# A two-layer transformer block on one core: the order of the jobs at the front of layer 0 and in the last expert run of layer 1

## The reference

```
h = layernorm(x) * (1 + ca) + sa
x = x + ga * attention(h)
h = layernorm(x) * (1 + cb) + sb
x = x + gb * experts(h)
```

```
for e in range(16):
    h = silu(xf @ W1[e] + b1[e]) * (xf @ W11[e] + b11[e])
    y = y + (h @ W2[e] + b2[e]) * gates[:, e, None]
z = silu(xf @ Ws1 + bs1) * (xf @ Ws11 + bs11) @ Ws2 + bs2
return y + z
```

## Time and profile before

| what | us |
|---|---|
| median of 3 executions | 1346.05 |
| lowest and highest of the 3 | 1339.43 and 1347.36 |
| the profiled execution, its own time | 1335.45 |
| its span, first to last instruction | 1333.7 |
| busy: PE, PEld | 973.1, 578.1 |
| busy: DVE, ACT, POOL | 844.6, 583.3, 437.7 |
| mean granted TensorE clock | 0.857 |

### The profile page before, as it was taken

One profiled execution on the slowest core, in us unless ns is written; L12 is line 12 of the kernel. 1 busy time (PEld: TensorE's weight loads), 2 busy tenths in 40 slices (PEclk: granted clock), 3 DMA queues, 4 the chain that ended last, 5 costly groups with the idle time before them and its releaser, 6 DMA issues.

```text
span 1333.7 us, 17366 instructions
## 1 busy us (share of the span) xinstructions
PE 973.1 (73%) x5741; PEld 578.1 (43%) x5741; DVE 844.6 (63%) x1977; ACT 583.3 (44%) x1409; POOL 437.7 (33%) x624
## 2 busy tenths in 40 slices
PE   5561374994985996887787888887877786877683
PEld 3231132452453564343334543444555553545573
DVE  1388888769989432566677656665655676635654
ACT  3334252453443243255454534434555553565253
POOL 0201342634635123022443232416312248423412
PEclk9775595996988998698799978768999997999787
DMA  7300000001000000000000000003144304242354
GB/s 229 102 0 0 1 0 1 1 0 36 1 1 1 0 1 25 23 1 0 1 1 1 1 0 1 1 0 129 55 116 125 87 25 148 77 123 66 129 179 119
DMA packets 54313, 60.40 MB, mean 45 GB/s; under 512 B 6208, under 2 KB 40656, under 8 KB 54224
## 3 DMA queue, kind: packets, MB, share of 16 engines
q1 hardware_dynamic: 52176, 55.10, 13.9%
q0 software_dynamic: 2048, 4.20, 1.1%
HBM read 46.05 MB, written 13.24 MB: 44 GB/s over the span
## 4 chain that ended last, share of the span: by engine, by line
PE 49%; DVE 21%; ACT 12%; issue 10%; POOL 6%; DMA 1%; SPq 0%; DVEq 0%; another core or an unknown queue 0%; POOLq 0%; ACTq 0%
PE banks L779 8%; PE banks L836 4%; PE banks L922 4%; PE banks L826 4%; DVE MX L1431 3%; PE banks L614 3%; PE banks L789 3%; POOL oms L1930 3%; PE banks L666 2%; PE banks L854 2%; PE banks L792 2%; PE banks L896 2%; ACT PT L1747 2%; ACT yh L1682 2%; PE banks L861 1%
## 5 line engine op out<-in xcount | busy, mean ns | idle before, releaser
L1431 DVE TENSOR_REDUCE MX<-banks 128x4 f32<-128x512 f32 (+2 forms) x192 | 199.2, 1043 | 89.6 <-PE banks L896 84.2
L1907 POOL TENSOR_SCALAR_AFFINE_SELECT PT<-PT 128x256 f32<-128x256 f32 x256 | 106.6, 430 | 405.5 <-ACT PT L1747 405.4
L1747 ACT ACTIVATE PT<-banks 128x768 f32<-128x768 f32 (+1 forms) x192 | 168.0, 878 | 108.1 <-PE banks L854 106.0
L779 PE MATMUL banks<-xgT,wg 128*128 128x128 f32 x616 | 87.8, 289 | 39.2 <-ACT ysb L1708 36.5
L861 PE MATMUL banks<-KS,QS 32*128 32x512 f32 (+3 forms) x512 | 98.0, 427 | 20.0 <-DVE MX L1431 15.7
L826 PE MATMUL banks<-w,hid 128*128 128x128 f32 x512 | 77.5, 299 | 45.2 <-DVE hid L1376 42.9
L922 PE MATMUL banks<-PT,VA 128*17 128x512 f32 (+3 forms) x1024 | 98.2, 483 | 16.2 <-DVE on L1454 10.8
L854 PE MATMUL banks<-QS,KS 32*128 32x128 f32 (+3 forms) x512 | 94.0, 412 | 14.1 <-ACT PT L1747 8.4
L826 PEld LDWEIGHTS banks<-w,hid 128*128 128x128 f32 x512 | 70.0, 207 | 78.8 <-DVE hid L1376 60.4
L779 PEld LDWEIGHTS banks<-xgT,wg 128*128 128x128 f32 x616 | 76.9, 197 | 51.9 <-issue 49.9
L1380 DVE SCALAR_TENSOR_TENSOR sil<-sil,yh 128x256 f32<-128x256 f32 x109 | 47.7, 438 | 62.5 <-ACT sil L1688 54.7
(11 more groups left out here) (273 smaller groups left out, 2100.2 us busy)
## 6 DMA issues: line engine op xcount, KB each, us to landing
wg<-in_ffn_dram SPq DMA_DIRECT2D x77, 386.0 KB
yb<-ysb SPq DMA_DIRECT2D x17, 256.0 KB, 3.9
xg<-xs SPq DMA_DIRECT2D x16, 256.0 KB
w<-in_ffn_w_dram SPq DMA_DIRECT2D x12, 256.0 KB
xs<-zt SPq DMA_DIRECT2D x2, 1472.0 KB, 14.2
xs<-zt SPq DMA_DIRECT2D x1, 1984.0 KB, 12.8
x<-in_L_attn_x_dram SPq DMA_DIRECT2D x4, 256.0 KB, 5.9
out_dram<-x SPq DMA_DIRECT2D x16, 64.0 KB
```

Of the source, the lines that this page charges most:

```text
L779: mm = e.matmul(ps[:, at:at + cols], w, h, start=True, stop=True)
L1431: v_mx.at(e.tensor_reduce(MX[n % 2][:, u:u + nm, qb % 2, 2 * pair:2 * pair + 2, 24].rearrange("p s i -> p i s"), p4, AX.X, ALU.max, negate ...
L1747: a_p.at(e.activation(PT[q % 3][:, 2 * pair:2 * pair + 2, :], where["score", q, pair][:, :, 0:n], ACT.Exp, scale=ISQ8))
L1907: ins = e.affine_select(out=pt, in_=pt, compare_op=ALU.is_ge, fill=0.0, base=0, pattern=[[0, 2], [1, 128]], channel_multiplier=-1)
```

## The change

At the front, `mod(1)` and the second group's jobs get other times, and `diag` is cut in three, each with its own signal: `diag(w)` writes four matrices, and `conv(g, w)` waits for w + 1 of them instead of for all. In the tail, the shared units 4 to 7 of the last batch move behind the first four tiles of the run, and the unit numbers and the banks follow. The gap in the table between chunk 0 and the other chunks grows from 6 to 10, and `turn(2, 0)` moves ahead on the scale.

```diff
@@ moe1_table
     for j in range(SHARED):
-        table += [(e + first + every * j, ("up", 1, n, j)), (e + first + 6.5 + every * j, ("down", 1, n, j))]
+        t = e + first + every * j if n < 3 or j < 4 else e + 70 + 2.1 * j
+        table += [(t, ("up", 1, n, j)), (t + 6.5, ("down", 1, n, j))]
...
-        gap = 6.0 if picked and c else 0.0
-        table.append((a - (2 if c != picked or not picked else 1.5) + step * tiles[0] + gap if c >= picked else e + 57,
+        gap = 10.0 if picked and c else 0.0
+        table.append((a - (2 if c != picked or not picked else 1.5) + step * tiles[0] + gap if c >= picked else e + 54.6,
@@ table_layer0
-    table = [(0.0, ("mod", 0)), (5.0, ("mod", 1))] + input_table(0, 1.0) + input_table(1, 6.0) + [(19.0, ("diag",))]
+    table = [(0.0, ("mod", 0)), (SCAN[0] + 1, ("mod", 1))]
+    table += [(1.0, ("stat", 0, 0, (0, 0))), (4.0, ("norm", 0, 0, (0, 0))), (5.0, ("stat", 0, 1, (0, 1))),
+              (7.2, ("norm", 0, 1, (0, 1)))]
+    table += [(8.0 + 4 * g + w, ("qkv", g, w)) for g in range(2) for w in range(3)]
+    table += [(12.5 + w, ("diag", w)) for w in range(3)] + [(24.0, ("ab", 0)), (28.0, ("ab", 1))]
@@ numbers of the units
-            return 16 * n + j if l == 0 else SHARED0[n] + j if j < SHARED else RUN0[n] + j - SHARED
+            if l == 0:
+                return 16 * n + j
+            if j >= SHARED:
+                return run_unit(n, j - SHARED)
+            return SHARED0[n] + j + (4 if n == 3 and j >= 4 else 0)
+
+        def run_unit(g, j):
+
+            return RUN0[g] + j - (4 if g == 2 and j < 4 else 0)
@@ conv on TensorE
-                pe.wait_ge(a_dg, 1)
+                pe.wait_ge(a_dg, w + 1)
@@ up on TensorE
-                    if j >= SHARED:
+                    if j >= SHARED and n < 2:
                         pool += (5,)
-                    i = pool[j % len(pool)]
+                    i = pool[(u if len(pool) == 5 else j) % len(pool)]
@@ diag on ScalarE
-            def diag():
+            def diag(w):
...
-                for j in range(12):
+                for j in range(4 * w, 4 * w + 4):
```

More of the change, by code:

```diff
@@ L498, in unit @@
         def unit(l, n, j):
-            return 16 * n + j if l == 0 else SHARED0[n] + j if j < SHARED else RUN0[n] + j - SHARED
+            if l == 0:
[5 more added lines that the diff above has]
+            return RUN0[g] + j - (4 if g == 2 and j < 4 else 0)
         def tile_unit(t):
             g = max(g for g in range(3) if TILE0[g] <= t)
-            return RUN0[g] + t - TILE0[g]
+            return run_unit(g, t - TILE0[g])
         def top_index(quarter, qb, u, pair):
@@ L1699, in turn @@
                     before, c0 = (g, c - 2) if c > 1 else (g - 1, len(CHUNKS[g - 1]) + c - 2)
-                    a.wait_ge(p_p3, RUN0[before] + CHUNKS[before][c0][-1] + 1)
+                    a.wait_ge(p_p3, run_unit(before, CHUNKS[before][c0][-1]) + 1)
                 a_xg.at(e.activation(xgT[cc % 2][:, 0:128 * m], where["turn", g, c][:, 0:128 * m], ACT.Copy))
@@ L1704, in keep @@
                 cc = CHUNK0[g] + j // 4
-                u = RUN0[g] + j
+                u = run_unit(g, j)
                 a.wait_ge(p_y, u + 1)
```

## The result

The changed kernel takes 1324.86 us in the median of 20 runs (1315.1 to 1332.53); the kernel before, measured with it, 1341.46 us in 20 runs (1329.09 to 1348.8). The ratio is 0.9888 with a 95% interval of 0.9865 to 0.9912, so 15.0 us less (11.8 to 18.1); the two medians are 16.6 us apart, the two means 15.0. Forecast were 18.1 us less and 1328 us. The profiled execution of the changed kernel has a span of 1322.9 us.

What follows compares the result with a forecast made beforehand. No engine is full; TensorE's serial jobs bound the front, idle time and low clock the tail. Front -7.6 and tail -10.5 sum to -18.1 us: 1328 from the 1346.05 median (profiled 1317.4), range 1317 to 1341.

Steps and rivals of the forecast that it cites:

- The front: Start of the kernel to the scan: convolutions' last transposes 10.6 us sooner, 3.0 given back, net 7.6 us less.
- the whole give-back: Behind the first scan step: VectorE waits for mod(1)'s products, delaying group 2's statistics and later scan steps; costs 3.0 us.
- B: Front: TensorE's clock stays low through all three convs, 5.9 us less gain, 1334 us in total; chance 0.12.
- D: Front: late x of group 1 or weights cw hold the chain, scan still pays 3.0; 1338.5 us; chance 0.09.
- The turn: Tail: turn(2, 0) goes with the parts of PT and ends at 1258.3 instead of 1263.87, 5.5 us sooner.
- The second half of the tail: From the turn's end to tile 8's `up`: 5 of the tail's 10.5 us, from filled idle time and faster clock.
- the other 5: Tail behind the turn: 3.12 us of idle time filled with work, and 1.9 us of clock on tiles 0 to 3.
- the 2.44 us: Tail: unexplained VectorE wait ahead of hid at 1268.65, taken to go with the second idle time.
- rival C: Tail: VectorE's wait returns, tiles 0 to 3 stay slow, a weight is late; 5.3 us less gain, 1333; chance 0.15.
- Rival E: Last run: with five banks, each tile's `up` waits for ScalarE's ysb; slower, up to 1353 us; chance 0.06.
- what would show it right: Front and tail marks: conv(0, 0) near 23, no 3 us idle, clock 1.00 behind the turn, tile 8's `up` 10.5 sooner.
- signs of being wrong: Front, scan and tail: convs of 5.4 us, `up` released by ysb, tiles waiting for weights, scan over 3.5 us longer.

Runs made afterwards that it cites:

- the turn alone: Changed kernel's front plus only the sooner turn(2, 0), all eight shared units ahead of tile 0 as before; mean 1324.1 us against 1341.3 for the kernel before.
- chips X and Z: Two follow-up groups, front or tail variants and unedited repeats, all profiles with stops; the changed kernel took 1340.3 and 1341.5 us, the kernel before 1346.9 and 1349.2.
- front alone: Only the front edits, with the tail of the kernel before: 1340.0 us against 1346.9 in one group, 1345.6 against 1349.2 in another.
- chip Y: Follow-up group of four kernels with the new front and sooner turn, no stops in their profiles: 1322.1 to 1325.7 us against 1341.3 for the kernel before.

## Why the prediction was right, and where it was not

**The front: right, term by term.** conv(0, 0) at 22.90 for a forecast of 22.85; its time 3.68 for 3.46; the last transposes at 37.75 for 37.7; VectorE's idle time 2.34, and the whole give-back 10.56 - 7.65 = 2.9 for 3.0. (The parts written down for the 3.0, products of 1.4 to 2.7 us and 0.55 us on VectorE from 73.94 on, give 1.5 to 2.8; that it met 2.9 is in part luck.) Over all profiles, step 45 is at 181.8 in the mean of nine with the new front and mod(1) as changed, and at 189.4 in three with the old: 7.6 us, the number forecast. Rivals B and D are out, by the convs of 3.7 and 3.5 us and by the start. Not tried was each of the three edits of the front by itself.

**The turn: right.** From the first operation on PT to xgT it is 6.83 us instead of 12.95, so 6.1 us for a forecast of 5.5, and at the low clock as expected; 0.5 us more were to be had with the clock.

**The second half of the tail: right in size, by luck, and wrong in its reason.** The forecast took 10.5 us to tile 8's `up`, and the first two profiles show 11.2 (11.57 less the 0.33 by which VectorE's first operation on PT came sooner); 10.5 are left at the last ysb, most of the difference being the wait for weights ahead of tile 13. The forecast had taken everything from tile 8 on as shifted; these 0.7 us are the exception. But the step that read "the other 5 are the second idle time of 3.12 that has work in it now, and 5.68 - 3.81 = 1.9 of clock" was not what happened. With the turn alone, in the old order of units, both are gone as well on a chip without stops, and 10.4 of the 11.3 us at the fifth ysb are there: 6.1 of the turn, 2.4 of a stop that did not come, 1.9 of clock. The step that failed is the sentence on the 2.44 us: "I can't explain; I let it go with the idle time". It was the trace of a stop: VectorE's hid waits there for TensorE's count p_y, which rises at 1268.53, where the records end the three `down` at 1266.07. And it does not go with the idle time: on chips X and Z the new order meets it with more behind it, and takes 38.2 us to the fifth ysb where the old one takes 36.6. There the tail part gains nothing: changed against front alone is +0.3 us in the means on X and -4.1 on Z, each with some 5 us of uncertainty, and +3.2 and +1.4 at equal clock. This is nearest to rival C, the wait that comes back, but by another way than C has it: not through VectorE's mixed queue, but as a stop of ScalarE ahead of tiles 1 and 2. Its price is 12.8 us at the fifth ysb instead of the 5.3 put on C.

**The sum.** 18.1 us forecast, 15.0 (11.8 to 18.1) measured. The 1328 us come near the measured 1324.9 also because the 1346.05 that they start from is 4.6 us above the median measured later. The first profile of the changed kernel has no stops, and its first runs take 1325.1 us in the mean, like the 1322.1 to 1325.7 of chip Y; on X and Z the same program takes 1340.3 and 1341.5. That the forecast was held against runs of the first kind is luck. The kernel before varies less, 1340.1, 1341.3, 1346.9 and 1349.2. On chip Y, the four kernels with the new front and the sooner turn lie 15.6 to 19.2 us below the kernel before, as forecast; on X and Z the change is worth 6.6 and 7.7 in the means, and 3.7 and 5.1 at equal clock. Rival E, an `up` that waits for its bank, did not come without stops: in the last run ysb releases no `up` of TensorE. With stops it does, once, for 2.1 to 4.7 us. The forecast's own list of what would show it right held where there were no stops; with stops, the clock of 1.00 in the 12 us behind the turn, the missing idle time and the 10.5 us did not. Of its signs of being wrong, a tile that waits for weights came, with the 0.66 us above, beside the waits that the kernel before has too.

## What to carry to other kernels

A wait in the profile that no job explains is not free to be dropped with the idle time around it: price the change with it gone, with it kept, and with it moved onto the new order's chain. Before a gain is credited to an order, run the order with one of its two edits: here, where there are no stops, the sooner turn alone gives all but 0.8 us. Where one stage swings by 20 us between executions, as the attention does here, read small effects as distances between marks in the stage that was changed, in several profiles, and not from the time.

## What the runs showed of the hardware

TensorE's completions can come late for its waiters though its own rows show the products in time: on chip X the records end tile 1's products at 1255.6, and the signal comes 6.5 us later. The stops stand just behind a burst of seven weight fetches beside a scatter (DMA share 0.97 in the 5 us ahead of the one on chip X) in nine of fourteen profiles, and the same nine have a second one between 906 and 926 us, 2.0 to 2.2 us on VectorE, which begins some 7 us behind the last fetch of a like burst. The burst alone is not enough: the first profile of the changed kernel has a share of 0.98 in its tail and no stop, nor has any on chip Y. The traces without stops hold more events too: 4020 to 4031 landings of transfers against 3194 to 3332 in the nine with stops. Whether the stop belongs to the recording or to the chip can't be told from that. The plain times speak rather for the chip: the changed kernel is 15 to 16 us slower on X and Z than in its first runs, and the kernel before beside it by only 7 to 9 (1340.1 against 1346.9 and 1349.2). The 7 to 8 us between the two come near the 10 that lie between the 12.8 and the 2.4 of the profiles. What causes the stops stays open. The attention stage took 673.9 to 694.6 us for the same instructions, TensorE's granted clock alone being different (0.89 and 0.86 in the shortest and the longest), and it follows neither of the two fronts.
